# Where the second normalised rows are transposed: TensorE and a stored copy, or transposing DMAs

## What is computed

```python
x = x + xattn(layernorm(x), ctx, pos, ...)     # 32 heads of 16, context of 256 features
h = layernorm(x).reshape(2048, 512)            # the "second normalised rows"
shared = swiglu(h, shared_w1, shared_w3, shared_w2)
scores = sigmoid(h @ gate_w.T)                 # 16 experts
_, topk = top_k(scores + bias, 2)              # gates: the two scores over their sum
routed = sum over e of combine[:, e:e+1] * swiglu(h, w1[e], w3[e], w2[e])
x = x + shared + routed
```

## Time and profile before

| | |
|---|---|
| time, median of 3 runs | 740.51 us (737.42 to 745.31) |
| time of the profiled execution | 740.43 us |
| its span, first to last instruction | 738.7 us |
| TensorE busy | 681.3 us, 92% of the span |
| VectorE busy | 525.3 us, 71% |
| ScalarE busy | 397.6 us, 54% |
| GpSimd busy | 366.1 us, 50% |
| mean clock granted to TensorE | 0.976 of full speed |

### The profile page before, as it was taken

One profiled execution on the slowest core, in us unless ns is written; L12 is line 12 of the kernel. 1 busy time (PEld: TensorE's weight loads), 2 busy tenths in 40 slices (PEclk: granted clock), 3 DMA queues, 4 the chain that ended last, 5 costly groups with the idle time before them and its releaser, 6 DMA issues.

```text
span 738.7 us, 20567 instructions
## 1 busy us (share of the span) xinstructions
PE 681.3 (92%) x7616; PEld 436.3 (59%) x7616; DVE 525.3 (71%) x992; ACT 397.6 (54%) x666; POOL 366.1 (50%) x439
## 2 busy tenths in 40 slices
PE   3389999999999999998489998999999999999992
PEld 1156666666666666666245665666666666666661
DVE  5968888888888888876537772467676666767671
ACT  4255666665666666665521111366666656666661
POOL 5455556655556665542100001145776557777662
PEclk9789999999999999999979999999999999999997
DMA  9610111000011110000113256258568875555952
GB/s 300 222 48 9 37 38 39 34 21 35 21 35 35 35 35 28 28 29 31 59 57 100 72 182 225 73 145 250 97 192 239 254 199 94 98 94 78 278 121 31
DMA packets 37601, 73.88 MB, mean 100 GB/s; under 512 B 3920, under 2 KB 8048, under 8 KB 37552
## 3 DMA queue, kind: packets, MB, share of 16 engines
q1 hardware_dynamic: 26736, 48.81, 19.2%
q0 software_dynamic: 8800, 20.73, 14.9%
q10 hardware_dynamic: 2016, 3.67, 1.7%
HBM read 69.85 MB, written 22.81 MB: 125 GB/s over the span
## 4 chain that ended last, share of the span: by engine, by line
PE 83%; DVE 6%; DMA 4%; issue 3%; POOL 2%; ACT 1%; POOLq 0%; SPq 0%; DVEq 0%; ACTq 0%
PE p_sc L712 13%; PE p_qk L692 13%; PE p_sc L692 12%; PE p_v L486 8%; PE p_qk L486 7%; PE p_pv L586 5%; PE p_st L534 4%; PE p_pv L589 4%; PE p_sc L566 3%; PE p_sc L549 3%; PE p_pv L596 2%; PE p_tr L678 2%; PE p_v L699 2%; PE p_sc L569 2%; DMA xeT<-xn2T_dram 2%
## 5 line engine op out<-in xcount | busy, mean ns | idle before, releaser
L809 ACT ACTIVATE prob<-p_sc 128x512 f32<-128x512 f32 x128 | 71.4, 601 | 58.8 <-PE p_sc L569 58.8
L1073 DVE TENSOR_REDUCE negmax<-p_sc 128x4 f16<-128x512 f32 x128 | 82.7, 685 | 8.6 <-PE p_sc L549 8.0
L924 ACT CAST hiddenT<-p_v 128x384 f16<-128x384 f32 x54 | 25.9, 479 | 108.7 <-PE p_v L699 108.7
L712 PE MATMUL p_sc<-used_twice,hiddenT 128*128 128x512 f16 (+1 forms) x342 | 80.1, 379 | 0.0
L1192 DVE TENSOR_TENSOR hidden<-p_sc,act_g 128x352 f32<-128x352 f32 x55 | 28.8, 524 | 68.5 <-PE p_sc L692 47.0
L1467 POOL COPY from_at<-from_rows 128x1 uint32 (+1 forms) x40 | 33.0, 825 | 89.0 <-DVE from_rows L1309 85.8
L692 PE MATMUL p_sc<-used_twice,xeT 128*128 128x352 f16 x468 | 76.2, 313 | 0.0
L692 PE MATMUL p_qk<-used_twice,xeT 128*128 128x352 f16 x468 | 76.2, 312 | 0.0
L1487 POOL DMA_INDIRECT out<-prob,to_at x38 | 67.8, 1786 | 11.0 <-issue 10.1
L1100 DVE SCALAR_TENSOR_TENSOR used_twice<-w,used_twice 128x704 f16<-128x704 f32 x80 | 67.7, 887 | 2.5
L692 PEld LDWEIGHTS p_sc<-used_twice,xeT 128*128 128x128 f16 x468 | 45.8, 98 | 24.0
(11 more groups left out here) (186 smaller groups left out, 1551.3 us busy)
## 6 DMA issues: line engine op xcount, KB each, us to landing
w<-e SPq DMA_DIRECT2D x20, 1408.0 KB
w<-e SPq DMA_DIRECT2D x20, 512.0 KB
out<-stream SPq DMA_DIRECT2D x17, 256.0 KB, 2.1
xn_dram<-xn_parts SPq DMA_DIRECT2D x16, 256.0 KB, 2.0
xn2T_dram<-xn2T SPq DMA_DIRECT2D x16, 256.0 KB, 2.0
w<-e SPq DMA_DIRECT2D x20, 192.0 KB
stream<-x SPq DMA_DIRECT2D x1, 3584.0 KB, 16.8
xeT<-xn2T_dram ACTq DMA_DIRECT2D x14, 256.0 KB, 2.7
```

Source lines behind the costliest of these rows:

```text
L712: mm = pe.matmul(p_y[u][:], hiddenT[0:k, h_part, c, :], w[0:k, w_part, c, :], start=(c == 0 and h_part + w_part == 0), stop=(c == len(ICH) ...
L809: act.activation(prob[:, c % RING, :], p_scored(c)[:], ACT.Exp, scale=SCALE).then_inc(exp_ready, 1)
L1073: dve.tensor_reduce(negmax[:, c % 2, at:at + CH], p_scored(c)[:].rearrange("p (h t) -> p h t", t=P), AX_X, ALU.max, negate=True).then_inc( ...
```

## The change

The eight transposes of `xn2_parts` on TensorE, ScalarE's copy of them out of PSUM and the store to `xn2T_dram` go, with that DRAM tensor. In their place SP issues a DMA that transposes while it copies: `turn_xn2` reads `xn2_parts` in SBUF (128 rows x 1024 float16) and writes `xn2T` in SBUF, right behind the store of the rows. `gate_logits` now waits for that DMA. In the shared stage `xeT` is filled by transposing DMAs that read the plain rows from `xn2_dram`: two on SP for tiles 0 and 1, fourteen on ScalarE's queue. ScalarE waits, before its first Silu, for all stores of rows and for the two loads of SP, so that the transposing DMAs of the two queues don't overlap. The DMA sizes stay at 256 KB each.

```diff
--- before.py
+++ after.py
@@ -91,7 +91,6 @@
 
 
         xn2_dram = nc.dram_tensor("xn2_dram", [T, 2 * DIM], F16, kind="Internal").ap()
-        xn2T_dram = nc.dram_tensor("xn2T_dram", [T, 2 * DIM], F16, kind="Internal").ap()
 
 
         stream = sb("stream", [P, B, DIM])
@@ -257,9 +256,9 @@
 
         attnT_hi = sem("attnT_hi"); attnT_lo = sem("attnT_lo"); gate_parts = sem("gate_parts")
         wo_done = sem("wo_done"); ln2_step = sem("ln2_step"); rstd2_ready = sem("rstd2_ready")
-        xn2T_done = sem("xn2T_done"); xn2T_ready = sem("xn2T_ready")
+        xn2T_ready = sem("xn2T_ready")
         xn2_hi = sem("xn2_hi"); xn2_lo = sem("xn2_lo")
-        xn2_stored = sem("xn2_stored"); xn2T_stored = sem("xn2T_stored"); gate_done = sem("gate_done"); logits_kept = sem("logits_kept")
+        xn2_stored = sem("xn2_stored"); gate_done = sem("gate_done"); logits_kept = sem("logits_kept")
 
         gate_exp = sem("gate_exp"); route = sem("route"); masks_ready = sem("masks_ready")
         counted = sem("counted"); experts_known = sem("experts_known"); slots_known = sem("slots_known")
@@ -398,11 +397,8 @@
                 sp.wait_ge(xn2_stored, b * 16 + 16)
                 sp.dma_start(xn2_dram[bass.ds(b * P, P)], xn2_parts[:, par].rearrange("p a d -> p (a d)")).then_inc(xn2_stored, 16)
 
-            def store_xn2T(b, par):
-                sp.wait_ge(xn2T_ready, b + 1)
-                if later(b, 1):
-                    sp.wait_ge(xn2T_stored, b * 16)
-                sp.dma_start(xn2T_dram[bass.ds(b * P, P)], xn2T[:].rearrange("p a c t -> p (a c t)")).then_inc(xn2T_stored, 16)
+            def turn_xn2(b, par):
+                sp.dma_start_transpose(xn2T[:].rearrange("p a c t -> p (a c) t"), xn2_parts[:, par].rearrange("p a d -> p (a d)")).then_inc(xn2T_ready, 16)
 
             def load_ctx(b, half):
                 if later(b, 2):
@@ -413,11 +409,11 @@
             def step(b, on):
                 on(4, load_ctx)
                 on(-1, store_xn2)
-                on(-1, store_xn2T)
+                on(-1, turn_xn2)
                 if isinstance(b, int) and b == B - 1:
-                    sp.wait_ge(xn2T_stored, 2 * 16)
+                    sp.wait_ge(xn2_stored, 3 * 16)
                     for n in range(2):
-                        sp.dma_start(xeT[:, n].rearrange("p a c t -> p (a c t)"), xn2T_dram[n * P:(n + 1) * P]).then_inc(sems.xT_loaded[n], 16)
+                        sp.dma_start_transpose(xeT[:, n].rearrange("p a c t -> p (a c) t"), xn2_dram[n * P:(n + 1) * P]).then_inc(sems.xT_loaded[n], 16)
 
             load_ctx(2, 0)
             load_ctx(3, 1)
@@ -610,20 +606,13 @@
                 if c == KC - 1:
                     mm.then_inc(wo_done, 1)
 
-            def xn2_transpose(b, par):
-                pe.wait_ge(xn2_lo, b + 1)
+            def gate_logits(b, par):
+                pe.wait_ge(xn2T_ready, b * 16 + 16)
 
                 last_xn = B if isinstance(b, int) and b + 4 > B else b + 4
                 pe.wait_ge(xnT_lo, last_xn)
                 if later(b, 1):
                     pe.wait_ge(logits_kept, b)
-                for a in range(2):
-                    for c in range(KC):
-                        mm = pe.transpose(p_xT[:, a, c, :], xn2_parts[:, par, a, c * P:(c + 1) * P], ident16[:])
-                mm.then_inc(xn2T_done, 1)
-
-            def gate_logits(b, par):
-                pe.wait_ge(xn2T_ready, b + 1)
                 if not later(b, 1):
                     pe.wait_ge(gate_parts, 2)
                 for c in range(KC):
@@ -637,7 +626,6 @@
                 on(-3, spread_recip, 1)
                 on(-1, project_q, 0)
                 on(-2, scores, 2)
-                on(-4, xn2_transpose)
                 on(-1, project_q, 1)
                 on(-2, scores, 3)
                 on(-1, project_q, 2)
@@ -820,19 +808,12 @@
                     act.wait_ge(wo_done, b)
                 act.copy(attnT[:, 0], attn_rows).then_inc(attnT_hi, 1)
 
-            def xn2T_copy(b, par):
-                act.wait_ge(xn2T_done, b + 1)
-                if later(b, 1):
-                    act.wait_ge(gate_done, b)
-                    act.wait_ge(xn2T_stored, b * 16)
-                act.copy(xn2T[:], p_xT).then_inc(xn2T_ready, 1)
-
             def xn2_high(b, par):
                 act.wait_ge(ln2_step, b * 5 + 5)
                 if later(b, 1):
                     act.wait_ge(xn2_stored, b * 16)
                 if later(b, 2):
-                    act.wait_ge(xn2T_done, b - 1)
+                    act.wait_ge(xn2T_ready, b * 16 - 16)
                 act.copy(xn2_parts[:, par, 0], xn2[:, par]).then_inc(xn2_hi, 1)
 
             def ctx_high(b, par):
@@ -870,7 +851,6 @@
             act.wait_ge(zeroed, 1)
 
             def step(b, on):
-                on(-5, xn2T_copy)
                 on(0, ctx_high)
                 on(-2, v_copy)
                 on(-3, exp, 0)
@@ -941,9 +921,11 @@
 
             def load_rows(n, u):
                 act.wait_ge(sems.u_done, n - 1)
-                act.dma_start(xeT[:, u].rearrange("p a c t -> p (a c t)"), xn2T_dram[n * P:(n + 1) * P]).then_inc(sems.xT_loaded[u], 16)
-
-            act.wait_ge(xn2T_stored, B * 16)
+                act.dma_start_transpose(xeT[:, u].rearrange("p a c t -> p (a c) t"), xn2_dram[n * P:(n + 1) * P]).then_inc(sems.xT_loaded[u], 16)
+
+            act.wait_ge(xn2_stored, B * 16 + 16)
+            for n in range(2):
+                act.wait_ge(sems.xT_loaded[n], 16)
             gate_act(0)
 
             def pair(j, par, kinds):
```

## The result

| | time, median (range), runs | ratio to before (95% interval) |
|---|---|---|
| before | 740.08 us (737.42 to 745.31), 13 | |
| after | 746.37 us (740.95 to 753.27), 13 | 1.0067 (1.0041 to 1.0094) |

The medians differ by 6.3 us, and the interval of the ratio is 3.0 to 7.0 us; the forecast was 739.1 us, a gain of 1.3. The cost lies inside the 1% that the forecast called "within", but its sign is measured.

A forecast was written before the change was run, and what follows sets the result against it. The prediction took TensorE, busy in 92% of the span and never idle in a steady attention step, as the bound. From 740.4 us, -4.7 (steps), +1.3 (end of stage), +2.1 (two loads) and 0 (twelve loads) gave 739.1 us, range 734 to 790.

The forecast's parts named there:

- within: Whole kernel: a time change of under 1% either way, held not measurable here; chance 0.49.
- What a transposing DMA takes: Each 256 KB transposing DMA: 3.1 us to landing from SBUF, 3.8 us from DRAM.
- Issue on ScalarE: Shared stage: issue longer than a plain load's 0.39 us would be covered by 3.60 us of ScalarE idle time.
- Steady attention steps: what comes late next: Attention steps: scores(3) starts 0.36 us earlier, then waits for VectorE's maxima; 13 steps gain 4.7 us.
- The rest of the step follows: Attention step after scores(3): the whole 0.36 us gain carries through, VectorE having 2.9 us to spare.
- a little more idle time costs no further clock: End of attention stage: first gate_up runs slowly, 3.70 us, either way, so longer idle time adds nothing.
- +1.3 at the end: End of attention stage: batch 15's transposing DMA lands 1.3 us later than transposes and copy did; bounds +0.2 to +5.5.
- Shared stage, +2.1 us: Two shared-tile loads beside the experts' weights, already late: 1.06 us extra each, 2.1 us; bounds 0 to 9.2.
- The twelve covered loads: Shared stage: twelve of fourteen loads have 3.75 us from issue to need, so 3.8 us landings cost 0.
- A: Shared stage: transposing loads outlast their 3.75 us cover, 15 us lost per us beyond; 758 to 792 us; chance 0.38.
- B: Transposing DMAs land like plain ones, 2.0 and 2.7 us, and steps gain the full 0.55 us; 733.5 us; chance 0.13.
- C: Each DMA's eight blocks go one after another, 11.1 us from SBUF, 16.7 from DRAM; 862 us; chance 0.08.

The follow-up runs named there:

- after_neg_first: The changed kernel with neg_copy put ahead of ln1_norm on VectorE; 744.68 us, ratio 1.0068 to the kernel before.
- turn_only: Changed kernel, gate's rows still turned by DMA, but xn2T stored to DRAM and the shared tiles loaded from it plainly; 742.36 us, ratio 1.0039 to the kernel before.
- rows_only: Kernel before, its gate transposes and copy kept, but shared tiles loaded by transposing DMAs from xn2_dram, no xn2T store; 741.81 us, ratio 1.0019.
- after_half: Changed kernel with new experts' w13 loads halved in the routed stage (output not the reference's); 741.10 us, against 739.29 for the kernel before halved likewise.
- before_third: The kernel before, unchanged, run again for a further profile; 740.07 us.
- after_again: The changed kernel, unchanged, run again for a second profile; 745.84 us, ratio 1.0095 to the kernel before.

## Why the prediction was wrong

A gain of 1.3 us was forecast and a loss of 6.3 measured. Of the sum, the term for the steady steps was too large, the one for the late loads of the shared stage too small, and TensorE's clock and the routed stage had no term at all.

- **What a transposing DMA takes: right.** 3.1 us from SBUF (3.1 forecast), 3.4 from DRAM (3.8). The shape of the estimate held too: the profile counts 14784 packets for fourteen of the DMAs, 1056 each, where the forecast had 1024 pieces. The 261 GB/s of the Trainium skill ("DMA: Bandwidth & Descriptors", "Latency and other measured facts"), which gave an estimate of 3.0 us from DRAM, was as near to the measured 3.4. The 1309 ns for one block (the Trainium skill, "VectorE: DVE Perf Modes", "The three transpose paths") does not apply eight times in a row to one DMA: as an estimate that would be 10.5 us, and 3.1 to 3.4 were measured.
- **Issue on ScalarE: right.** 1.25 us instead of 0.39, under the 3.60 us of idle time.
- **"Steady attention steps: what comes late next", -4.7 us: mis-sized.** `scores(3)` came 0.34 earlier. The sentence that failed is "The rest of the step follows". VectorE has 2.9 us to spare in a step, but not at that place: `ln1_norm` moved further under GpSimd's second operation, took 1.42 instead of 1.08 us and held `neg_copy`, which the next scores need. The term measured -1.94; `after_neg_first`, at 19.72 us a step, shows that the order on VectorE alone caused the difference.
- **"a little more idle time costs no further clock": wrong.** That clause was right for the first `gate_up`, 3.70 us either way. But the granted clock was lower at 340 to 350 us in five profiles of six (and in `turn_only`, not in `rows_only`). In these five the lead over the kernel before shrank there by 0.8 to 2.2 us, and in `after_half` by nothing. The last batch's output product took 5.32 us against 2.76 in the profile of before, which is scatter: `before_third` has 5.30 too. Together with +1.3 at the end, which was right, the stage comes out at 373.99 - 113.39 = 260.60 us against 259.79, so +0.8 instead of -3.4. Against `before_third`, with its 260.32, it is +0.3, which is -1.94 + 0.9 + 1.3; on average over six profiles after the change and four before it is +0.5.
- **Shared stage, +2.1 us: right in place, small in size.** The twelve covered loads cost at most 0.4 us. With the two beside the weights the stage took 105.6 to 109.6 us over four profiles against 103.7 to 105.5 over four of the kernel before: 3.4 more on average. In `after_again` the two landings are 13.61 us in sum against 12.99 and 12.52, about 1 more. In the other three profiles, with a first landing of 7.7 to 8.0 us, the clock falls as well, which costs up to 2.6 more. No term of the sum had that. The fall isn't the transposing loads' alone: it came in `turn_only` behind a plain load.
- **No term for the routed stage: the largest failure.** The forecast took a stage that the change doesn't touch as unchanged. By the halved loads 2.6 to 4.5 us of the 6.3 went there: gathers that land late, TensorE's wait of 3.3 to 3.9 us for one of them, and the fall of its clock. Attention and shared stage by the profiles (0.5 and 3.4) and this add up to more than 6.3; the timed runs with halved loads put the first two at 1.8 to 2.2 together, so the four profiles show the dear form of the shared stage more often than the timed runs do, as far as can be told.
- **Rivals.** A was rightly told by its condition, the landing against 3.75 us, and did not occur; a landing of 4.1 us at one tile cost 0.3 us. B had the landings of plain DMAs, 2.0 and 2.7 us, and C 11.1 and 16.7; both are out by the same rows. None of the three named the clock or a queue further down. The measured 746.37 us lies inside the stated range by luck, since the slower side was there for A, whose mechanism played no part.

## What to carry to other kernels

When an operation leaves the critical engine, follow the next consumer's whole chain on the other engine in the order of its queue: spare time somewhere in a step is no spare time behind an operation that now runs beside another engine's. A wait of TensorE can cost more than its length, because the matmuls behind it may run at half the clock: here waits of 1.9 to 4.0 us did so in some profiles and not in others. And work that was priced at nothing because a wait covered it may still have shortened TensorE's idle time. Where loads land late beside other large ones, compare distributions of runs and lighten those loads in both kernels before a change is credited with what happens there.

## What the runs showed of the hardware

- A transposing DMA of 256 KB took 1.25 to 1.32 us of its queue to issue (medians), three to four times a plain one's 0.33 to 0.39.
- The same VectorE operation (128x512 float32, L976) took 0.54, 1.08 and 1.42 us as a tensor operation of GpSimd ran beside it for 0.11, 0.80 and 1.14 us.
- TensorE's granted clock fell to 1.2 GHz beside idle times of 1.89 us (`turn_only`) to 3.99 us (`after`) in the shared stage, and stayed at 2.4 GHz behind 2.89 us (`after_again`) and 3.20 us (`after_neg_first`).
- Halving one load of 1.4 MB per new expert took the upper half of the run times away: 737.3 to 740.6 us over 12 runs, against 738.7 to 748.5 over 22 runs of the kernel before in the same session (a 23rd took 907.7).
